# q and k with tokens on the partitions, head sums along the free axis

## What is computed

```python
x = x + attn(_layernorm(x))
x = x + ffn(_layernorm(x))
# attn
q = (x @ Wq + bq).reshape(b, s, 16, 8)            # k and v alike
q = _layernorm(q, q_scale, q_bias)                # over the 8 features of a head
scores = jnp.einsum('bqhd,bkhd->bhqk', q, k) * 8 ** -0.5
out = jnp.einsum('bhqk,bkhd->bqhd', softmax(scores), v).reshape(b, s, 128) @ Wo + bo
# ffn, with int32 weights times 1/127
h = silu(x @ w_gate.T) * (x @ w_up.T);  out = h @ w_down.T
```

## Time and profile before

| | us |
|---|---|
| median of 3 runs | 439.92 (438.5 to 441.55) |
| profiled execution, first to last instruction | 437.3 |
| ahead of turn 0 | 45.4 |
| turn 0 up to the start of turn 1 | 36.6 |
| turn 1 | 51.8 |
| each of turns 2 to 5 | 47.8 |
| tail, after the last product with v | about 23 |

### The profile page before, as it was taken

The page is one execution under the profiler, slowest core; times in us unless marked ns, Lnnn a source line. Parts: engine busy times, 40 slices in busy tenths (PEclk is TensorE's granted clock), DMA queues, the critical chain, the costliest instruction groups (busy, mean ns, idle before and its releaser), DMA issues.

```text
span 437.3 us, 7192 instructions
## 1 busy us (share of the span) xinstructions
PE 401.8 (92%) x2338; PEld 174.0 (40%) x2383; DVE 242.3 (55%) x607; ACT 288.6 (66%) x322; POOL 49.0 (11%) x65
## 2 busy tenths in 40 slices
PE   4774799799999999999999999999999999999966
PEld 4553122144343533354344444253434434323345
DVE  5797118048825694459724892569545880243054
ACT  2111789677768677777677777868777777886601
POOL 7500002002002200210020200220020101020010
PEclk9956799899999999999999999999999999999979
DMA  3208505900465027600654045601750055500000
GB/s 102 46 28 214 89 0 166 150 1 1 145 110 110 1 73 169 113 7 0 184 112 63 0 139 100 120 0 41 185 108 1 0 167 105 90 2 0 26 1 24
DMA packets 32943, 32.74 MB, mean 75 GB/s; under 512 B 3608, under 2 KB 29848, under 8 KB 32920
## 3 DMA queue, kind: packets, MB, share of 16 engines
q1 hardware_dynamic: 32056, 32.19, 32.6%
q10 hardware_dynamic: 864, 0.26, 0.3%
HBM read 17.76 MB, written 14.68 MB: 74 GB/s over the span
## 4 chain that ended last, share of the span: by engine, by line
PE 76%; DVE 7%; ACT 7%; DMA 4%; issue 3%; SPq 2%; POOL 1%; ACTq 0%; POOLq 0%; DVEq 0%
PE scores L688 24%; PE oacc L702 23%; PE side L670 8%; ACT probs L559 6%; PE side L614 5%; PE side L677 4%; PE side L630 3%; PE side L643 3%; DMA kst<-parts_dram 2%; PE side L635 2%; DVE xn L864 1%; PE side L661 1%; DMA parts_dram<-parts 1%; PE scores L782 1%; SPq L349 1%
## 5 line engine op out<-in xcount | busy, mean ns | idle before, releaser
L559 ACT ACTIVATE probs<-scores 128x1024 f32<-128x1024 f32 x256 | 256.5, 1024 | 92.9 <-PE scores L688 92.4
L688 PE MATMUL scores<-qst,kst 128*128 128x512 bf16 x467 | 143.1, 387 | 14.1 <-DMA kst<-parts_dram 8.8
L702 PE MATMUL oacc<-probs,vaug 128*32 128x512 f32 x1024 | 137.1, 608 | 0.1
L688 PEld LDWEIGHTS scores<-qst,kst 128*128 128x128 bf16 x512 | 38.4, 99 | 150.8 <-issue 88.0
L702 PEld LDWEIGHTS oacc<-probs,vaug 128*32 128x32 f32 x1024 | 20.2, 108 | 55.3 <-issue 47.5
L461 POOL TENSOR_SCALAR ve<-mv 128x4 f32<-128x4 f32 (+1 forms) x17 | 3.9, 232 | 328.6 <-DVE mv L858 294.1
L1034 DVE TENSOR_TENSOR y<-side,x 128x512 f32<-128x512 f32 x7 | 4.8, 691 | 51.3 <-PE side L677 51.3
L864 DVE TENSOR_SCALAR xn<-x_in,mv,rs 128x128 f32<-128x128 f32 x32 | 19.1, 807 | 11.1 <-POOL rs L463 11.1
L942 DVE TENSOR_TENSOR qk_n<-side,qk_c 128x512 f32<-128x512 f32 x16 | 10.3, 685 | 20.9 <-PE side L614 20.9
L677 PEld LDWEIGHTS side<-wdT,hT 128*128 128x128 f32 x168 | 21.0, 192 | 2.0
L670 PE MATMUL side<-x2T,wuT 128*128 128x512 f32 x42 | 21.4, 592 | 0.0
(11 more groups left out here) (128 smaller groups left out, 380.0 us busy)
## 6 DMA issues: line engine op xcount, KB each, us to landing
parts_dram<-parts SPq DMA_DIRECT2D x24, 256.0 KB, 2.5
qst<-parts_dram SPq DMA_DIRECT2D x32, 192.0 KB, 4.9
kst<-parts_dram SPq DMA_DIRECT2D x32, 192.0 KB, 5.4
parts_dram<-parts SPq DMA_DIRECT2D x8, 384.0 KB, 2.6
parts_dram<-parts SPq DMA_DIRECT2D x24, 128.0 KB, 2.1
x_in<-in_L_attn_x SPq DMA_DIRECT2D x8, 256.0 KB, 3.7
x_res<-in_L_attn_x SPq DMA_DIRECT2D x8, 256.0 KB, 5.4
out_dram<-y SPq DMA_DIRECT2D x8, 256.0 KB, 2.0
```

Of the source, the lines that this page charges most:

```text
L559: act.activation(probs[:, kt, 2 * c:2 * c + 2, :], scores[:, 2 * c:2 * c + 2, :], ACT.Exp)\
L688: last = pe.matmul(scores[:, 2 * c + parity, :], kst[:, pair, kt * P:(kt + 1) * P], qst[:, pair, parity, :], start=True, stop=True)
L702: last = pe.matmul(oacc[STRIP * j:STRIP * (j + 1), :], vaug[:, kt, NG * g + j, :], probs[:, kt, j, :], start=first, stop=last_of_half)
```

## The change

q and k are made as v is: four products of 128 tokens each, tokens on the partitions. Their biases become rows beside v's, loaded as 128 x 128 blocks and centred together with the weights (768 values a partition in place of 512), so that the two matmuls for centred bias columns, the mask `group8` and `center` go. The side piece a_var goes, and with it its eight products. VectorE sums the squares of q, k and v in one instruction over 1536 values, and makes `hv` in one instruction. `rsqrt_end` ends with a plain third Newton step over all 192 factors; `hyx` goes. `normed` first multiplies q and k by their factors, tokens still on the partitions; a_rq and a_rk, in the same place, transpose this product, and VectorE applies scale and bias to the transposed result in PSUM. The banks of a_rq and a_rk are therefore free when `qk_f` is made.

The diff, cut to its core (left out: semaphores, buffers and masks that go, and renamed buffers):

```diff
-SIDE = {1: ["a_xT"], 2: ["b_OT1", "a_q"], 3: ["b_onT", "a_k"], 4: ["b_Wo", "a_v"], 5: ["a_var"],
+SIDE = {1: ["a_xT"], 2: ["b_OT1", "a_q"], 3: ["b_onT", "a_k"], 4: ["b_Wo", "a_v"],
         6: ["b_x2T"], 7: ["b_g0"], 8: ["a_rq", "a_rk"], 9: ["b_u0", "b_g1"], 10: ["b_u1", "c_OT0"],
         11: ["b_g2", "b_u2"], 13: ["b_d0"], 14: ["b_d1"]}
-BANK = {"a_xT": 0, "b_OT1": 1, "a_q": 2, "b_onT": 0, "a_k": 1, "b_Wo": 2, "a_v": 0, "a_var": 1,
+BANK = {"a_xT": 0, "b_OT1": 1, "a_q": 2, "b_onT": 0, "a_k": 1, "b_Wo": 2, "a_v": 0,
         "b_x2T": 2, "b_g0": 0, "a_rq": 1, "a_rk": 2, "b_u0": 1, "b_g1": 2, "b_u1": 0, "c_OT0": 1, "b_g2": 2,
         "b_u2": 0, "b_d0": 1}
 
 LAST_SLOTS = {6: [], 7: ["b_x2T"], 8: ["b_g0"]}
 SIDE_ORDER = [p for u in range(NU) for p in SIDE.get(u, []) if p != "b_d1"]
 PHASE_PIECES = {
-    "before": ["a_xT", "a_v", "a_q", "a_k", "a_var", "a_rq", "a_rk"],
+    "before": ["a_xT", "a_v", "a_q", "a_k", "a_rq", "a_rk"],
     "first": [p for p in SIDE_ORDER if p[0] != "b"],
     "loop": SIDE_ORDER,
     "last": [p for p in SIDE_ORDER if p[0] != "a"],
 }
 
 
-EARLY = ["a_xT", "a_q", "a_k", "a_v", "a_var"]
+EARLY = ["a_xT", "a_q", "a_k", "a_v"]
...
-        group8 = sb("group8", [P, P])
-        center = sb("center", [P, P])
-        wraw = sb("wraw", [P, 4, D])
-        head_sum = sb("head_sum", [P, 4 * NH])
-        wqkv = sb("wqkv", [P, 4, D])
-        bias_col = sb("bias_col", [P, 2])
-        bias_cen = sb("bias_cen", [P, 2])
+        wraw = sb("wraw", [P, 6, D])
+        head_sum = sb("head_sum", [P, 6 * NH])
+        wqkv = sb("wqkv", [P, 6, D])
...
-        qk_c = sb("qk_c", [P, 2, S])
-        qk_sq = sb("qk_sq", [P, 2, S])
-        v_c = sb("v_c", [P, NT, D])
-        v_sq = sb("v_sq", [P, NT, D])
-        v_sum = sb("v_sum", [P, NT * NH])
+        qkv_c = sb("qkv_c", [P, 3, NT, D])
+        qkv_sq = sb("qkv_sq", [P, 3, NT, D])
+        head_sq = sb("head_sq", [P, 3 * NT * NH])
         hv = sb("hv", [P, 3, NT, NH])
         hy = sb("hy", [P, 3, NT, NH])
         ht = sb("ht", [P, 3, NT, NH])
-        hyx = sb("hyx", [P, 2, NT, NH, HD])
-        qk_n = sb("qk_n", [P, 2, S])
+        qk_n = sb("qk_n", [P, 2, NT, D])
...
-                    "var": (hv_done, 2, 0), "rq": (qkn_done, 2, 0), "rk": (qkn_done, 2, 1),
+                    "rq": (qkf_done, 2, 0), "rk": (qkf_done, 2, 1),
...
-            act.dma_start(wraw[:, 3, :], bv_d.rearrange("(a n) -> a n", a=1).broadcast_to((P, D)))\
-               .then_inc(w_loaded, 16)
-            for k, src in enumerate((bq_d, bk_d)):
-                act.dma_start(bias_col[:, k:k + 1], src.rearrange("(p a) -> p a", a=1)).then_inc(bias_loaded, 16)
+            for k, src in enumerate((bq_d, bk_d, bv_d)):
+                act.dma_start(wraw[:, 3 + k, :], src.rearrange("(a n) -> a n", a=1).broadcast_to((P, D)))\
+                   .then_inc(w_loaded, 16)
...
-                    act.activation(qk_sq[:, w, :], qk_c[:, w, :], ACT.Square).then_inc(qksq_done, 1)
+                    act.activation(qkv_sq[:, w, :, :], qkv_c[:, w, :, :], ACT.Square).then_inc(qksq_done, 1)
...
-            pe.wait_ge(filled, 4)
+            pe.wait_ge(filled, 3)
             for _ in range(WARM_UP):
                 pe.matmul(scores[:, 3, 0:P], ident[:, :], ident[:, :], start=True, stop=True)
-            pe.wait_ge(consts, 1)
-            pe.wait_ge(bias_loaded, 32)
-            for k in range(2):
-                last = pe.matmul(scores[:, 0, k:k + 1], center[:, :], bias_col[:, k:k + 1], start=True, stop=True)
-            last.then_inc(bias_filled, 1)
-
             def prepare_later_weights():
-                pe.wait_ge(bias_centred, 1)
...
-                elif what in ("q", "k"):
-                    pe.wait_ge(xnT_done, b + 1)
-                    w = 0 if what == "q" else 1
-                    pe.matmul(bank, wqkv[:, w, :], xnT[:, :], start=True, stop=True)\
-                      .then_inc(q_filled if what == "q" else k_filled, 1)
-                elif what == "v":
+                elif what in ("q", "k", "v"):
                     pe.wait_ge(xnT_done, b + 1)
                     for t in range(NT):
-                        last = pe.matmul(bank[:, t * D:(t + 1) * D], xnT[:, t * P:(t + 1) * P], wqkv[:, 2, :],
-                                         start=True, stop=True)
-                    last.then_inc(v_filled, 1)
-                elif what == "var":
-                    for w in range(2):
-                        pe.wait_ge(qksq_done, 2 * b + w + 1)
-                        for t in range(NT):
-                            o = (w * NT + t) * NH
-                            last = pe.matmul(bank[:, o:o + NH], qk_sq[:, w, t * P:(t + 1) * P],
-                                             group8[:, 0:P:HD], start=True, stop=True)
-                    last.then_inc(var_filled, 1)
+                        last = pe.matmul(bank[:, t * D:(t + 1) * D], xnT[:, t * P:(t + 1) * P],
+                                         wqkv[:, "qkv".index(what), :], start=True, stop=True)
+                    last.then_inc({"q": q_filled, "k": k_filled, "v": v_filled}[what], 1)
                 elif what in ("rq", "rk"):
 
                     w = 0 if what == "rq" else 1
-                    pe.wait_ge(rsqrt_done, 3 * b + w + 1)
-                    transposes(bank, lambda t: hyx[:, w, t, :, :])\
-                        .then_inc(r_filled, 1)
+                    pe.wait_ge(qkn_done, 2 * b + w + 1)
+                    transposes(bank, lambda t: qk_n[:, w, t, :]).then_inc(r_filled, 1)
...
             def centred(b, w):
                 name, sem_f = (("a_q", q_filled), ("a_k", k_filled))[w]
                 dve.wait_ge(sem_f, b + 1)
-                dve.tensor_scalar(qk_c[:, w, :], side[:, BANK[name], :], bias_cen[:, w:w + 1], None, ALU.add)\
+                dve.tensor_tensor(out=qkv_c[:, w, :, :],
+                                  in0=side[:, BANK[name], :].rearrange("p (t d) -> p t d", t=NT),
+                                  in1=wqkv[:, 3 + w, :].unsqueeze(1).broadcast_to((P, NT, D)), op=ALU.add)\
                    .then_inc(qkc_done, 1)
 
             def centred_v(b):
                 dve.wait_ge(v_filled, b + 1)
                 at_least(dve, vaugB_done, b)
-                dve.tensor_tensor(out=v_c[:, :, :],
+                dve.tensor_tensor(out=qkv_c[:, 2, :, :],
                                   in0=side[:, BANK["a_v"], :].rearrange("p (t d) -> p t d", t=NT),
-                                  in1=wqkv[:, 3, :].unsqueeze(1).broadcast_to((P, NT, D)), op=ALU.add)\
+                                  in1=wqkv[:, 5, :].unsqueeze(1).broadcast_to((P, NT, D)), op=ALU.add)\
                    .then_inc(vc_done, 1)
 
             def variances(b):
                 dve.wait_ge(vsq_done, b + 1)
-                dve.reduce_sum(v_sum[:, :], v_sq[:, :, :].rearrange("p t (h d) -> p (t h) d", d=HD), AX.X)\
-                   .then_inc(vsum_done, 1)
-                dve.wait_ge(var_filled, b + 1)
-                dve.tensor_scalar(hv[:, 0:2, :, :].rearrange("p w t h -> p (w t h)"),
-                                  side[:, BANK["a_var"], 0:2 * NT * NH], HEAD_EPS, None, ALU.add)\
-                   .then_inc(hv_done, 1)
-                dve.wait_ge(vsum_done, b + 1)
-                dve.tensor_scalar(hv[:, 2, :, :].rearrange("p t h -> p (t h)"), v_sum[:, :], 1.0 / HD, HEAD_EPS,
+                dve.wait_ge(qksq_done, 2 * (b + 1))
+                dve.reduce_sum(head_sq[:, :], qkv_sq[:, :, :, :].rearrange("p w t (h d) -> p (w t h) d", d=HD), AX.X)\
+                   .then_inc(headsq_done, 1)
+                dve.wait_ge(headsq_done, b + 1)
+                dve.tensor_scalar(hv[:, :, :, :].rearrange("p w t h -> p (w t h)"), head_sq[:, :], 1.0 / HD, HEAD_EPS,
                                   ALU.mult, ALU.add).then_inc(hv_done, 1)
 
-                dve.wait_ge(hv_done, 2 * (b + 1))
+                dve.wait_ge(hv_done, b + 1)
                 dve.tensor_scalar(hy[:, :, :, :].bitcast(I32), hv[:, :, :, :].bitcast(I32), -0.5, RSQRT_SEED,
                                   ALU.mult, ALU.add).then_inc(seed_done, 1)
                 dve.wait_ge(seed_done, b + 1)
@@ -918,33 +868,28 @@
                 step(dve.tensor_tensor(out=t_all, in0=y_all, in1=y_all, op=ALU.mult), 1)
                 step(dve.scalar_tensor_tensor(out=t_all, in0=t_all, scalar=-0.5, in1=v_all,
                                               op0=ALU.mult, op1=ALU.mult), 2)
+                last = dve.scalar_tensor_tensor(out=y_all, in0=t_all, scalar=1.5, in1=y_all, op0=ALU.add, op1=ALU.mult)
                 if k < 2:
-                    step(dve.scalar_tensor_tensor(out=y_all, in0=t_all, scalar=1.5, in1=y_all,
-                                                  op0=ALU.add, op1=ALU.mult), 3)
+                    step(last, 3)
+                else:
+                    last.then_inc(rsqrt_done, 1)
 
             def rsqrt_end(b):
                 newton_step(b, 1)
                 newton_step(b, 2)
 
-                n = NT * NH
```

(24 more changed lines are left out.)

## The result

| | before | after |
|---|---|---|
| median of the runs, us | 439.21 (437.82 to 441.55, 4 runs) | 449.51 (449.28 to 449.66, 4 runs) |
| span of the profiled execution, us | 437.3 | 447.4 |
| distance of one turn to the next in the loop, us | 47.80 to 47.87 | 49.15 to 49.24 |

The changed kernel takes 1.0228 times as long, with a 95% interval of 1.0183 to 1.0272. The last line of the table is read from the timeline of VectorE: the starts of the additions that write a turn's result lie so far apart (the last distance, into the tail, is 42.34 in both kernels).

The account below looks back on a forecast made before the run. TensorE's list and VectorE's chain were taken to bound a turn together; 0.4 ahead of the loop, 8.5 in six turns and 1.6 for the clock gave +10.5 us on 439.92: 450.4 us, range 445 to 457.

Parts of the forecast that it names:

- Two bounds at once: Loop turn: TensorE's list and VectorE's chain both bind, with no slack at b_g0, so the deleted 1.69 us becomes waiting.
- The terms of a turn: Loop turn: copy of x2T 1.14 us later, transposes of qk_n 1.4 later; turn 47.8 to 49.2, six turns +8.5.
- The products of q and k: TensorE, loop turn: eight 128-column passes at 0.89 us replace two of 512 at 0.86, +0.03 each for q and k.
- Ahead of the loop: Before turn 0 +1.15 us (longer weight centring, long sum, exposed transposes), turn 0 itself -0.8; together +0.4.
- The clock: TensorE's granted clock falls in two of seven gaps (six loop stalls, start of turn 1), one more than now: +1.6 us.
- the second rival: Loop stalls occur but the clock stays up: 447 to 449 us; chance 0.71 together with the forecast.

Follow-up runs that it names:

- idle sum: Kernel before, with VectorE also summing the 1024 squares of q and k into an unread spare tile behind v's sum: 446.97 us, ratio 1.0148.
- cut sum: Changed kernel with its 1536-element sum split: q and k's 1024 squares summed ahead of x2n, v's 512 behind it: 443.36 us, ratio 1.0063.
- reordered kernels: Changed kernel, sum split, copy of x2T earlier, q/k transposes one unit later: 441.42 us; also with x2n transposes and first gate one unit later: 445.45 us.
- all takers one unit later: Changed kernel with VectorE reordered and transposes of q, k and x2n and first gate product each one unit later: 445.45 us, ratio 1.0132.

## Why the prediction was right, and where it was not

**Two bounds at once: right.** The decisive step was that b_g0 has no slack, read from one weight load 0.12 us behind the copy. The idle sum in the kernel before (turn +1.13 for 1.21) and the deleted matmuls without the sum (turn unchanged) show both halves of it apart from each other.

**The terms of a turn: right.** The sum was put at 1.75 us and took 1.742 on average over eight; the stalls at 0.8 and 2.0, and they are 0.69 and 1.62 by the brackets (1.8 by the starts: the gate matmul begins 2.22 us after the two score matmuls ahead of it, at 303.93, where it was 0.44 before). The copy was to end 1.14 late and does so by 1.06. Up to the transposes of k the prediction added a further 0.26 (1.4 less 1.14), for the second qk_n. That wait is there too: in the changed kernel the loads for k start at 309.68, 0.12 behind the second qk_n, and the way past the transposes has grown by 0.26 (the weight loads are shown at the cut sum). The turn was put at 49.2 and takes 49.18; six times 1.4 is 8.4, where the sum has 8.5. The group of the sum:

```profile
L848 DVE TENSOR_REDUCE head_sq<-qkv_sq 128x192 f32<-128x1536 f32 x8 | 13.9, 1742 | 1.2 <-POOL qkv_sq L444 1.2
```

**The products of q and k: right.** The chain of one loop turn has two rows of this kind, for q and k:

```profile
289.36 0.89 PE side L599 x8
...
292.65 0.89 PE side L599 x8
```

That is 0.11 us for a pass of 128 columns, against 0.43 for 512 before: here a pass costs by its columns. The section "Back-to-back issue gap" of the Trainium skill's "TensorE: Matmul & The Clock Gate" has about 81 ns at 128 columns and 131 ns at 512; the prediction's estimate from these figures, 2.5 us more a turn for the split, is not borne out by these fp32 passes.

**Ahead of the loop: wrong, +3.76 for +0.4.** Three pieces of the step were mis-sized.
First, the start of qk_n moved from 28.49 to 29.27, +0.78 where the terms gave -0.1 (0.53 + 0.4 - 1.04). The 24 passes for v, q and k took 5.46 us in one stretch, where the 12 passes of before took 4.53 (14.18 to 18.71); the prediction had no term for this. The split is not the reason: in the kernel without the 16-column matmuls the 12 passes of before took 5.43.

```profile
14.73 5.46 PE L599 MATMUL side<-wqkv,xnT 128*128 128x128 f32 x24 [1.42 <-DVE xnT L826]
```

```profile
14.27 2.04 PE L635 MATMUL side<-wqkv,xnT 128*128 128x128 f32 x8 [0.89 <-DVE xnT L875]
16.11 3.59 PE L630 MATMUL side<-xnT,wqkv 128*128 128x512 f32 x4
```

What differs is how long TensorE stayed slow. With ten warm-up matmuls, 12 passes took 4.34 to 5.43 us in four executions and 24 passes 4.54 to 5.46 in six, so that this piece isn't the change's own for certain either. From qk_n to the first part it is +1.42 for +1.25, in part since an affine step out of PSUM takes 0.81 and not 0.75.
Second, from the first part to turn 0 it is +1.0 for 0: the last store of parts landed after 3.72 us, not 2.14 as before. In the second profile of the changed kernel the store took 2.43 and the piece 14.83, as in the second of before (14.82). Over the executions seen, a store issued before 36.5 us landed in 2.1 to 2.3, and one issued after 37 in 2.4 to 3.8; what it meets there stays open.
Third, turn 0 was to be 0.8 shorter and is 0.56 longer (0.48 between the second profiles). Turn 0 begins later, and by windows of 1 us its granted clock is 0.50 up to 54, 5.4 us from the turn's start, where before it was 0.50 up to 48, 2.6 us from the start. The transposes of q and k begin 19.8 us after the turn's start (68.38) instead of 18.6 (64.02), and of that 1.2 the shorter work behind them gives back only 0.7. This too isn't the change's own for certain: the kernels with the idle sum and without the 16-column matmuls have turn 0 of before as it was, and took 37.6 and 39.0 us for it, where before took 36.6 and 36.3.
The failed step is thus the one that summed this stretch from a single execution of before, with TensorE as fast and the store as quick as they were there, and put nothing for either. How much of the 2.3 to 3.8 us is the change and how much the execution, no run here separates.

**The clock: wrong in size and sign, +1.6 for -1.6.** I took a fall in two of seven gaps. There is none in the six stalls of the loop, in either profile of the changed kernel, and the one at turn 1 is gone in both. (The 51.8 us for turn 1 in the table of before don't measure the price of a fall: they run to the second product with v of turn 2. From the first, at 82.33, to the first, at 131.50, it is 49.2.) This was the term of the second rival, and as a mechanism the rival was the better one: stalls, with the clock up.

**Why the total fits all the same.** Of the span: +3.8 ahead of the loop (0.4 forecast), +8.3 in six turns (8.5 forecast), -1.6 for the clock (+1.6 forecast), -0.4 in the tail: +10.1 against +10.5. The two misses are each over 3 us and cancel. The sign and the size of the main term come from the step that was right; that the total came within 1 us of the median is partly luck.

**Not seen at all.** With the change, a bank of transposes is read out by the affine step, not by the product ahead of it. In the changed kernel a unit lies between that bank's release and its next taker and hides it; the reordered kernels paid for it (b_u0's wait, 0.47 and 0.60). The prediction named when the banks come free and found it enough, but did not say that slack is used up there.

## What to carry to other kernels

Work taken off the busiest engine is a gain only as far as its next wait can end earlier; look for the last load or matmul that starts within 0.1 or 0.2 us of its producer, for there a second engine bounds the turn, however low its busy share. Such a change should come with new dates for both sides: the takers in the consumer's list, and the order of the producer's list for these dates, with a unit left between the release of a buffer and its next writer. A first-in-order instruction that waits holds up everything behind it, so a longer instruction belongs where its engine waits anyway.

## What the runs showed of the hardware that I had not expected

The granted clock after a stall at the start of turn 1 does not follow from the stall's length alone. It fell after idle times of 2.46 (before), 2.17 (its second profile), 2.69 (without the 16-column matmuls), 2.65 (longer warm-up), and also of 1.77 in the kernel with the cut sum; it stayed up after 1.86 and 1.32 (the changed kernel's two profiles), 1.62 and 1.50 (the two reordered ones), and also after 2.30 in the kernel with the idle sum. The rows of two that speak against a simple rule, the kernel with the idle sum and the one with the cut sum:

```profile
83.14 0.60 PE L689 MATMUL scores<-qst,kst 128*128 128x512 bf16 x2 [2.30 <-DMA kst<-parts_dram]
83.67 1.07 PE L703 MATMUL oacc<-probs,vaug 128*32 128x512 f32 x8
```

```profile
85.42 0.60 PE L643 MATMUL scores<-qst,kst 128*128 128x512 bf16 x2 [1.77 <-DMA kst<-parts_dram]
85.95 1.63 PE L657 MATMUL oacc<-probs,vaug 128*32 128x512 f32 x8
```

In the loop no stall of up to 1.8 us brought the lower level. Each fall costs about 1.6 us here, so that this much of a single comparison of spans can be chance.

The 24 passes ahead of turn 0 took 4.54 to 5.46 us in six executions with ten warm-up matmuls and 2.92, 4.26 and 4.54 in three with 32. The longer warm-up likely shortens this stretch, but the two sets touch, and even the shortest, at 0.12 us a pass, is only just the price that the loop pays always.

In this stretch the granted clock of the rows does not tell TensorE's pace. One microsecond of it, before and after, with six passes in each:

```profile
15.00:16.00 1.00, 1.00 (x6) 1.00 (x6) 1.00 (x8) 0.00 (x0) 0.00 (x0) 1.00 0.04 0
```

```profile
15.00:16.00 1.00, 1.00 (x6) 1.00 (x6) 0.95 (x8) 0.00 (x0) 0.00 (x0) 0.50 0.04 0
```

The rows say 1.00 for before and 0.50 for after, and the passes take the same 0.23 us each, twice the 0.11 of the loop. In the kernel with all takers one unit later the rows stay at 1.00 throughout, and its 24 passes took 5.46 us all the same. Ahead of the loop the durations of like matmuls are the safer measure.
